# Edge tiles of a relational graph convolution: read from one packed copy, or from the four input arrays

## The reference

```python
def _L0_gnn_ref(h, weight, norm, src, dst, rel_type):
    transformed = jnp.einsum('ni,rio->rno', h, weight)
    msg = transformed[rel_type, src] * norm
    return jax.ops.segment_sum(msg, dst, num_segments=h.shape[0])

x = _layernorm(x + _L0_gnn_ref(x, L0_gnn_weight, edge_weight1, src, dst, edge_type_16), axis=-1)
```

## Time and profile before

| what | us |
|---|---|
| median of 3 runs | 2512.22 (2507.72 to 2512.82) |
| the profiled execution's own time | 2488.83 |
| its span, first to last instruction | 2487.1 |
| PE busy in the span | 2151.0 (86%) |
| DVE / ACT / POOL busy in the span | 1227.0 / 270.3 / 1536.9 |

### The profile page before, as it was taken

The page is one execution under the profiler, slowest core; times in us unless marked ns, Lnnn a source line. Parts: engine busy times, 40 slices in busy tenths (PEclk is TensorE's granted clock), DMA queues, the critical chain, the costliest instruction groups (busy, mean ns, idle before and its releaser), DMA issues.

```text
span 2487.1 us, 33329 instructions
## 1 busy us (share of the span) xinstructions
PE 2151.0 (86%) x11962; PEld 1950.8 (78%) x11962; DVE 1227.0 (49%) x3388; ACT 270.3 (11%) x557; POOL 1536.9 (62%) x1649
## 2 busy tenths in 40 slices
PE   3688988898988888988888888888988988889889
PEld 2578887887877778887887788788877878878788
DVE  2554554545454545454554454545555454545444
ACT  0211110111110111111111111111111110111101
POOL 6566666666666666666666666666666666666660
PEclk7799999898999999999999898999999989998989
DMA  4433333333333333333333333333333333333330
GB/s 144 138 92 97 96 98 97 92 94 98 96 94 95 97 93 96 92 101 92 96 98 98 92 98 93 99 95 97 95 99 96 94 96 93 96 95 98 92 94 27
DMA packets 107712, 238.97 MB, mean 96 GB/s; under 512 B 31226, under 2 KB 55642, under 8 KB 107482
## 3 DMA queue, kind: packets, MB, share of 16 engines
q0 software_dynamic: 77760, 212.43, 29.9%
q1 hardware_dynamic: 29342, 21.02, 2.8%
q10 hardware_dynamic: 440, 3.32, 0.3%
HBM read 230.23 MB, written 9.72 MB: 96 GB/s over the span
## 4 chain that ended last, share of the span: by engine, by line
PE 78%; issue 12%; DVE 5%; another core or an unknown queue 2%; ACT 1%; DMA 1%; SPq 0%; POOL 0%; POOLq 0%; ACTq 0%
PE ps_a L988 54%; PE ps_z L947 15%; PE ps_z L949 8%; DVE a_lo L757 1%; DVE spread L791 1%; PE ps_m L931 1%; ACT a_hi L862 1%; DVE below L791 0%; DVE w_raw L791 0%; DMA w_raw<-in_L_gnn_weight 0%; DVE z_stat L739 0%; DVE z_rows L737 0%; POOL rows L560 0%; DVE z_rows L747 0%
## 5 line engine op out<-in xcount | busy, mean ns | idle before, releaser
L560 POOL DMA_INDIRECT rows<-in_x,idx x1614 | 1528.7, 947 | 893.6 <-issue 408.5
L988 PE MATMUL ps_a<-spread,rows 128*128 128x96 f32 (+7 forms) x5700 | 1165.0, 336 | 183.5 <-issue 133.3
L988 PEld LDWEIGHTS ps_a<-spread,rows 128*128 128x128 f32 x5700 | 945.4, 204 | 285.5 <-issue 176.9
L947 PE MATMUL ps_z<-w_parts,a_hi 128*128 128x512 f32 x1568 | 843.5, 539 | 46.2 <-issue 31.7
L757 DVE TENSOR_TENSOR a_lo<-ps_a,a_hi 128x512 fp32r<-128x512 f32 x392 | 251.6, 684 | 1094.0 <-ACT a_hi L862 787.8
L791 DVE TENSOR_SCALAR spread<-ps_i,key,meta 128x192 f32<-128x192 f32 (+8 forms) x1290 | 518.6, 465 | 26.2 <-remote 14.6
L949 PE MATMUL ps_z<-w_parts,a_lo 128*128 128x256 f32 x1568 | 457.6, 292 | 35.3 <-issue 34.9
L862 ACT ACTIVATE a_hi<-ps_a 128x512 fp32r<-128x512 f32 x392 | 212.3, 593 | 2005.9 <-PE ps_a L988 1535.8
L947 PEld LDWEIGHTS ps_z<-w_parts,a_hi 128*128 128x128 f32 x1568 | 316.3, 202 | 68.6 <-issue 45.3
L949 PEld LDWEIGHTS ps_z<-w_parts,a_lo 128*128 128x128 f32 x1568 | 316.1, 202 | 47.6 <-issue 44.8
L988 PE MATMUL ps_a<-w_raw,rows 128*128 128x208 f32 (+7 forms) x1452 | 287.7, 326 | 34.1 <-issue 29.3
(11 more groups left out here) (75 smaller groups left out, 249.7 us busy)
## 6 DMA issues: line engine op xcount, KB each, us to landing
rows<-in_x,idx POOLq DMA_INDIRECT x1614
xr<-in_x SPq DMA_DIRECT2D x48, 128.0 KB
out<-z_rows SPq DMA_DIRECT2D x48, 128.0 KB
w_raw<-in_L_gnn_weight SPq DMA_DIRECT2D x16, 256.0 KB
raw<-packed SPq DMA_DIRECT2D x192, 20.0 KB
packed<-in_src ACTq DMA_DIRECT2D x1, 805.7 KB
packed<-in_dst ACTq DMA_DIRECT2D x1, 805.7 KB
packed<-in_edge_type ACTq DMA_DIRECT2D x1, 805.7 KB
```

The source lines that it names most:

```text
L560: pool.indirect_dma_start(rows[:, row, :], None, x, bass.IndirectOffsetOnAxis(ap=index, axis=0)).then_inc(arrived, 16)
L947: pe.matmul(zk, a_hi[:, ak, h, r, :], w_parts[:, r, h, :, :].rearrange("p a f -> p (a f)"), start=n == 0, stop=False, skip_group_check=True)
L988: ins = pe.matmul(ps_a[:, g % OPEN, h, (begin - zero) * R:(stop - zero) * R], rows[:, step.row, h * P:(h + 1) * P], spread_at(n)[:, (begin ...
```

## The change

The packed copy of all edges goes. For blocks 1 to 47 SyncE issues, for each part, four transfers, one from each input array, where it issued one from `packed`; the register is read once for each part as before. ACT's queue fills a small tensor `ending` with the last 8106 edges and the padding; only the last block reads from it, with one transfer for each part, and SP waits for it just ahead of that block. So that no read runs past the inputs, DVE limits the first edges: those of the first 188 parts from above, those of the last 4 from below, and these become offsets into `ending`. Then it counts bounds that were moved by this and adds 2^20 for each to `total`, so that the general path would run. ACT waits for 256 counts of `edges_in` per block in place of 64.

```diff
-    packed = nc.dram_tensor("packed", [4, E + PART_EDGES], I32, kind="Internal").ap()
+    ending = nc.dram_tensor("ending", [4, TAIL + PART_EDGES], I32, kind="Internal").ap()
...
-                    first = sp.value_load(first_i[0:1, n:n + 1], min_val=0, max_val=E)
-                    sp.dma_start(raw[PT * s:PT * s + PT, :, :],
-                                 packed[:, bass.ds(first, PART_EDGES)].rearrange("a (j p) -> j a p", p=P)).then_inc(
-                                     edges_in, 16)
+                    if b == NB - 1:
+
+                        first = sp.value_load(first_i[0:1, n:n + 1], min_val=0, max_val=TAIL)
+                        sp.dma_start(raw[PT * s:PT * s + PT, :, :],
+                                     ending[:, bass.ds(first, PART_EDGES)].rearrange(
+                                         "a (j p) -> j a p", p=P)).then_inc(edges_in, 64)
+                    else:
+                        first = sp.value_load(first_i[0:1, n:n + 1], min_val=0, max_val=LAST_FIRST)
+                        for a, v in enumerate((src, dst, rel, norm_i)):
+                            sp.dma_start(raw[PT * s:PT * s + PT, a, :],
+                                         v[bass.ds(first, PART_EDGES)].rearrange("(j p) -> j p", p=P)).then_inc(
+                                             edges_in, 16)
...
             sp.wait_ge(first_edges_ready, 1)
-            sp.wait_ge(edges_packed, 8 * 16)
             raw_left(1)
...
                 if b + 3 < NB:
+                    if b + 3 == NB - 1:
+                        sp.wait_ge(ending_filled, 8 * 16)
                     raw_left(b + 3)
...
-                dve.tensor_scalar(first_i[0:1, :], first_near[0:1, :], float(P), None, ALU.mult).then_inc(
-                    first_edges_ready, 1)
+                EARLY, LATE = slice(0, BOUNDS - GROUPS), slice(BOUNDS - GROUPS, BOUNDS)
+                done(dve.tensor_scalar(first_cut[0:1, EARLY], first_near[0:1, EARLY], float(LAST_FIRST // P), None,
+                                       ALU.min))
+                done(dve.tensor_scalar(first_cut[0:1, LATE], first_near[0:1, LATE], float(ENDING // P), None, ALU.max))
+                done(dve.tensor_scalar(first_i[0:1, EARLY], first_cut[0:1, EARLY], float(P), None, ALU.mult))
+                dve.tensor_scalar(first_i[0:1, LATE], first_cut[0:1, LATE], float(P), float(ENDING), ALU.mult,
+                                  ALU.subtract).then_inc(first_edges_ready, 1)
+                dve.wait_ge(first_edges_ready, 1)
+                done(dve.tensor_tensor(first_cut[0:1, :], first_cut[0:1, :], first_near[0:1, :], ALU.not_equal))
+                done(dve.reduce_sum(cut[0:1, :], first_cut[0:1, :], axis=AX_X))
+                done(dve.scalar_tensor_tensor(out=total[0:1, :], in0=cut[0:1, :], scalar=float(1 << 20),
+                                              in1=total[0:1, :], op0=ALU.mult, op1=ALU.add))
...
-                wait(act, edges_in, b, 64, 64)
+                act.wait_ge(edges_in, 64 + 256 * b)
...
-            def pack_edges():
+            def fill_ending():
                 for a, v in enumerate((src, dst, rel, norm_i)):
-                    act.dma_start(packed[a, 0:E].rearrange("(p e) -> p e", p=PACK),
-                                  v.rearrange("(p e) -> p e", p=PACK)).then_inc(edges_packed, 16)
+                    act.dma_start(ending[a, 0:TAIL].rearrange("(p e) -> p e", p=6),
+                                  v[ENDING:E].rearrange("(p e) -> p e", p=6)).then_inc(ending_filled, 16)
```

More of the change, by code:

```diff
@@ L113, in build @@
     SC = SROWS // SP
-    PACK = 125
     BOUNDS = PARTS - GROUPS
@@ L118, in build @@
     PAD_DST = 1 << 19
+    TAIL = E % P + 63 * P
+    ENDING = E - TAIL
+    LAST_FIRST = (E - PART_EDGES) // P * P
     assert CT <= BT and GROUPS % OPEN == 0 and PARTS == GROUPS * NB
-    assert SROWS * SROW == E and SP * SC == SROWS and 2 * HALF == BOUNDS <= 192 and E % PACK == 0
+    assert SROWS * SROW == E and SP * SC == SROWS and 2 * HALF == BOUNDS <= 192
     plan = [[Step(t, t, first, end, [(g, max(first, g * GN), min(end, (g + 1) * GN)) for g in range(GROUPS)
@@ L231, in build @@
         first_i = sb("first_i", [1, BOUNDS], I32)
+        cut = sb("cut", [1, 1])
         tiles_row = sb("tiles_row", [1, BOUNDS])
@@ L312, in build @@
                                              for n in range(2 * SROW, 2 * SROW + 3 * BOUNDS, BOUNDS))
+        first_cut = first_tile
         over_below = below.rearrange("p c b -> p (c b)")
@@ L363, in build @@
         samples_in = sem("samples_in")
-        edges_packed = sem("edges_packed")
+        ending_filled = sem("ending_filled")
         padding_made = sem("padding_made")
@@ L841, in copy_edges @@
                                ACT.Copy).then_inc(edges_copied, 1)
-            def pack_edges():
+            def fill_ending():
                 for a, v in enumerate((src, dst, rel, norm_i)):
-                    act.dma_start(packed[a, 0:E].rearrange("(p e) -> p e", p=PACK),
-                                  v.rearrange("(p e) -> p e", p=PACK)).then_inc(edges_packed, 16)
+                    act.dma_start(ending[a, 0:TAIL].rearrange("(p e) -> p e", p=6),
+                                  v[ENDING:E].rearrange("(p e) -> p e", p=6)).then_inc(ending_filled, 16)
                 act.wait_ge(padding_made, 2)
                 for a in range(4):
-                    act.dma_start(packed[a, E:E + PART_EDGES].rearrange("(p e) -> p e", p=64),
-                                  pad_i[:, int(a == 1), :]).then_inc(edges_packed, 16)
+                    act.dma_start(ending[a, TAIL:TAIL + PART_EDGES].rearrange("(p e) -> p e", p=64),
+                                  pad_i[:, int(a == 1), :]).then_inc(ending_filled, 16)
             def evacuate(part):
@@ L890, in fast_scalar @@
             copy_edges(0)
-            pack_edges()
+            fill_ending()
             blocks(act, tile_block)
```

## The result

The changed kernel takes 2530.21 us (median; 2526.87 to 2534.52). The kernel before, run beside it, takes 2512.52 us (2507.72 to 2513.75). The ratio is 1.008, with a 95% interval of 1.0062 to 1.0098: 17.7 us slower by the medians. The forecast was 2518.2 us with a range up to 2526: the sign was right, the size three times too small.

A forecast was written before the change was run, and what follows sets the result against it. PE bounds the kernel (78% of the span), with SyncE's issue time on the path in the first 110 us. -4.9 + 0.85 + 5.0 + 5.0 = +6.0 us on 2512.2 gives 2518.2 us, range 2507 to 2526.

The forecast's parts named there:

- The body, costed at 0: Later blocks: edge loads issue 5 us longer, SyncE keeps 16 us of slack, edges are used a block later; cost 0.
- its test: Body of the trace: nothing should differ; the prediction is wrong if the body's PE share moves.
- small transfers be coalesced: Skill rule against 24 extra transfers: 48 us at 2.0 us each one after another; set aside because issues overlap.
- The gain of 4.9 us: Search at the start: without the copy's contention the `dst` fetch lands sooner, PE's turn at 22.3 against 27.2 us.
- The 0.85 us on DVE: Search at the start: three more DVE instructions ahead of the `first_i` semaphore, 0.28 us each, 0.85 us on the path.
- Block 1 and block 2, 5.0 us each: Start: extra issues delay weight 2 behind block 1's load, and block 2's edges for ACT; +5.0 us each.
- The pitch of 0.42 us: SyncE's queue: each extra edge transfer takes 0.42 us to issue, twelve a block, 5.0 us a block.
- the dearest end: SyncE's queue: upper bound for an extra transfer's issue, 1.06 us each, 12.7 us a block.
- The gain doesn't arrive: Rival, start: something the change doesn't touch ends DVE's stall and swallows the 4.9 us; +10.9 us, 2523.1 us, chance 0.20.
- The sign set for it: Start of DVE's L653: still near 55.9 us means the gain is swallowed; below 45 us means the stall is gone.
- the stall goes away with the copy: Rival, start: DVE goes on at about 22.8 instead of 55.85 us; -22.2 us, 2490.0 us, chance 0.14.
- The transfers issue slowly: Rival, SyncE at the start: extra transfers take 1.06 us each; +21.4 us, 2533.6 us, chance 0.07.

The follow-up runs named there:

- h_body: Kernel before, with only blocks 4 to 47 loaded by four transfers a part from the input arrays, copy still made: 2497.56 against 2483.41 us, 1.006.
- rows5x2: Kernel before, with blocks 4 to 47 loaded by five transfers a part (two tiles, all four arrays) from the packed copy: 2526.82 against 2512.09 us, 1.0058.
- split8: As h_body, but each of a part's four transfers cut in two, 28 extra issues a block: 2496.03 us against 2483.33 us of the kernel before, 1.0059.
- copy_kept: The changed kernel, with the copy of all edges still made but read by nobody: 2500.59 us against 2483.41 us of the kernel before, 1.0076.
- pool_held: Kernel before, but GpSimd's gathers of block 0 wait ahead of tile 12 until `first_i` is there: 2484.75 against 2483.41 us, 1.0006.

## Why the prediction was wrong

**The body, costed at 0, cost 14.2 us.** This is the step that failed: "5 us more leave 16 us. The edges themselves are used a block later. Cost: 0." Its premises hold: the slack is there (in blocks 5 to 46 at least 10.1 us in `h_body` and 5.2 us in `rows5x2` are left between an edge load and the next output rows), and the load still ends long before it is used. The conclusion doesn't, since it took SyncE's time for the only price of a transfer. Twelve idle transfers of 16 rows a block, which nobody waits for, already cost 1.0032; 24 register moves cost nothing.

By what means a transfer from SyncE slows PE stays open. The table of stretches, whose PE row the prediction had named as its test, is a weak one for 0.6%; here it is of `h_body` and, below, of `split8`, which lost as much:

```profile
400.00:2400.00 2000.00, 1768.19 (x9831) 1604.04 (x9830) 991.30 (x2648) 213.28 (x442) 1260.31 (x1333) 0.92 0.34 95
```

```profile
400.00:2400.00 2000.00, 1755.07 (x9837) 1587.79 (x9836) 996.30 (x2661) 212.33 (x443) 1259.81 (x1331) 0.94 0.33 95
```

Against the earlier trace rows PE's busy time in `h_body` is the same within 0.1%, and only the count of its instructions shows the loss: 9831 in place of 9879 in the same 2000 us, 0.5% fewer. So its matmul rows got longer, 179.9 ns in the mean against 179.1, together 7 us, at a granted clock of 0.92 against 0.93; its idle time is only 1.6 us more. In `split8` it is the other way round: rows of 178.4 ns at 0.94, and 15 us more idle time. Over all runs the mean granted clock says the same. It is lower than before in `h_body` (0.9127 against 0.9228) and `copy_kept` (0.9145 against 0.9228) and higher in `split8` (0.9265 against 0.9219) and `rows5x2` (0.9293 against 0.9182), with about the same loss. A lower clock can be a part of the loss in some of these kernels; it isn't what they have in common.

Nor does the delay stand beside the issues. Worked out from PE's rows of before and `h_body` over blocks 5 to 46, a block takes 49.67 in place of 49.44 us, which over 44 blocks is 10 us. PE is 1.2 us late (standard error 0.4 us) already at the turn of the edges, ahead of which the next load can't go out, and behind it makes up all but 0.2 us by the block's end.

The Trainium skill's rule in "DMA: Bandwidth & Descriptors", section "Rules for kernel authors", that small transfers be coalesced, which the prediction set aside, was right in its direction, though not by a fixed part paid one after the other.

**The gain of 4.9 us didn't come.** Its first half was right in kind: the fetch took 2.68 us (2.73 forecast), and the turn came 3.0 us earlier, not 4.9, since GpSimd came to the fetch 1.7 us later than before (17.71 us against 15.99). Its second half, that the end of the search sets what follows, was wrong. `copy_kept`, where the search is slower again, moves the first weight by 2.3 us and shows no loss beside the change, and `pool_held` shows that GpSimd's gathers, not the search, set when SyncE, DVE and PE go on.

**The 0.85 us on DVE.** From L666's start to `first_i`'s end 2.18 us now, 1.20 us before: 0.98 us. It lies inside the time that the gathers take anyway; no run has it alone.

**Block 1 and block 2, 5.0 us each.** All three blocks of the start together cost 5.6 us (1.0024; by its interval 3.0 to 8.9 us), not 10.0. The pitch of 0.42 us was right where no gathers run; where they do, one transfer took 2 to 3 us. Sixteen issues took 30.0 us (31.36 to 61.36) in place of the 9 that were forecast, dearer than the dearest end, and it hardly mattered, since that time was lost before, too. At block 2, ACT's wait did grow as forecast, but block 2 alone gives 1.0003, though PE waits 7.16 us there: a wait that gets longer at one place of PE need not be there at the end. Where it is made up isn't shown.

**The rivals.** "The gain doesn't arrive" was right, and for the reason it gave (gathers without a wait to 50.75 us). The sign set for it was not: L653 no longer starts at 55.9 us but at 26.5, by which the faster rival, "the stall goes away with the copy", should have held. The stall had only gone to SyncE's queue. "The transfers issue slowly" forecast 2533.6 us, near the result, but by 24 issues on the path at 1.06 us, with nothing in the body; that is not what happened, and the nearness is luck. What the forecast lacked was any case with a price in the body.

**The sum by the runs:** removing the copy 0 as far as measured, the start +5.6, the body +14.2, in all 19.8 us. Measured were 17.2 us with `copy_kept` and 17.7 with the change itself, whose intervals both hold 19.8.

## What to carry to other kernels

Slack on the issuing queue doesn't make a transfer free: beside a PE that is busy throughout, 12 more small transfers in each of 44 blocks cost 14 to 18 us where they carried the edges and 4 to 13 us where nobody waited for them, so merge small loads, even at the price of one copy ahead. When a long wait stands with "remote" and another engine streams without a wait beside it, look whether engines that don't wait for each other tick at the same slow pitch; if so, shortening the waiting chain only moves the stall. Name for each step the time at which what follows it starts, not the time at which the step itself starts: L653 moved by 29 us and the weights by 1.

## What the runs showed of the hardware

- Beside a stream of row gathers that GpSimd issues back to back (one in 1.25 us), DVE and SyncE come to start instructions in steps of 0.70 us: a MEMSET every 0.7 to 2.1 us in place of 0.025 us, an edge transfer in 2 to 3 us in place of 0.4. It doesn't begin with the stream (DVE ran freely up to 32.8 us beside one from 18.98 us on, and up to 30.8 us beside one from 27.77 us on), and it ends 4 to 5 us after the last gather (5.1, 5.0 and 3.8 us in three kernels).
- Further SyncE transfers cost time on a PE-bound stretch without anyone waiting for them: 1.0016 with 12 of one row a block, 1.0032 to 1.005 with 12 or 24 of 16 rows, 1.0058 to 1.0072 where the edge load itself is cut into 16 to 32. Between the last two groups the intervals overlap, so that carrying data makes a transfer dearer isn't shown.
- The loss levels off: 4 extra edge transfers a block 1.0014, 12 to 28 of them 1.0058 to 1.0072.
